# Relation lookups of a graph network on one Trainium2 core: one-hots in bfloat16 and a table in three bfloat16 parts

## The reference, cut to what matters

```python
half = N_REL // 2
is_fwd = edge_type < half
ridx = jnp.where(is_fwd, edge_type, edge_type - half)
for l in range(N_LAYERS):                       # 2 layers
    comp = x[src] * rel_emb[l][ridx]            # float32, 64 wide
    agg_f = jax.ops.segment_sum(comp * norm * fmask, dst, num_segments=N_NODES)
    agg_b = jax.ops.segment_sum(comp * norm * bmask, dst, num_segments=N_NODES)
    x = agg_f @ w_fwd[l] + agg_b @ w_bwd[l] + x @ w_loop[l]
    x = jax.nn.relu(x)
```

## Time and profile before

| | us |
|---|---|
| median of 3 runs | 11818.08 |
| lowest, highest | 11797.62, 11822.92 |
| the profiled execution's own time | 11901.01 |
| span of the program in it | 11899.2 |
| TensorE busy in the span (57%) | 6783.1 |
| GpSimd busy (51%) | 6085.0 |
| VectorE busy (36%) | 4232.3 |
| ScalarE busy (17%) | 1966.8 |

### The profile page before, as it was taken

The page is one execution under the profiler, slowest core; times in us unless marked ns, Lnnn a source line. Parts: engine busy times, 40 slices in busy tenths (PEclk is TensorE's granted clock), DMA queues, the critical chain, the costliest instruction groups (busy, mean ns, idle before and its releaser), DMA issues. The chain is left out here.

```text
span 11899.2 us, 136950 instructions
## 1 busy us (share of the span) xinstructions
PE 6783.1 (57%) x37299; PEld 5699.3 (48%) x37300; DVE 4232.3 (36%) x12350; ACT 1966.8 (17%) x5277; POOL 6085.0 (51%) x6396
## 2 busy tenths in 40 slices
PE   3554555556444445666666666676555555545454
PEld 3554544455322324555555555555455555444444
DVE  4333322222211113444444444444334333333333
ACT  1222200001211121111112111111211111111111
POOL 4666656665466653444443444444344444355554
PEclk6555556555667666666666666666655555566566
DMA  4444423232233322333332333333222222233333
GB/s 122 142 140 137 134 68 78 76 78 63 73 73 74 74 70 88 103 103 103 103 103 87 103 104 104 104 104 102 63 74 76 75 75 75 60 95 95 96 94 83
DMA packets 774628, 1092.78 MB, mean 92 GB/s; under 512 B 389184, under 2 KB 429440, under 8 KB 774160
## 3 DMA queue, kind: packets, MB, share of 16 engines
q0 software_dynamic: 233760, 503.07, 17.3%
q1 hardware_dynamic: 540784, 588.70, 16.5%
HBM read 1016.16 MB, written 75.04 MB: 92 GB/s over the span
## 5 line engine op out<-in xcount | busy, mean ns | idle before, releaser
L681 POOL DMA_INDIRECT gat_rows<-xw_table,gat_index x2736 | 2592.0, 947 | 3118.1 <-DVE gat_msg_s L1748 1971.9
L1834 PE MATMUL bank<-gat_msg_s,gat_hot 128*128 128x264 f32 (+1 forms) x5472 | 1942.7, 528 | 28.6 <-DVE gat_msg_s L1748 16.3
L1811 PE MATMUL bank<-gat_ends_s,gat_hot 128*128 128x9 f32 x5472 | 1153.2, 350 | 1183.1 <-issue 857.8
L1811 PEld LDWEIGHTS bank<-gat_ends_s,gat_hot 128*128 128x128 f32 x5472 | 1137.0, 316 | 1319.8 <-issue 950.0
L1834 PEld LDWEIGHTS bank<-gat_msg_s,gat_hot 128*128 128x128 f32 x5472 | 1430.8, 303 | 296.3 <-issue 31.0
L681 POOL DMA_INDIRECT att_rows<-pre_table,att_index x912 | 862.5, 946 | 830.1 <-ACT att_index L671 478.9
L681 POOL DMA_INDIRECT msg_rows<-pre_table,msg_index x912 | 864.8, 948 | 651.0 <-ACT msg_index L671 385.1
L681 POOL DMA_INDIRECT gcn_rows<-in_x,gcn_index x912 | 878.6, 963 | 573.8 <-ACT gcn_index L671 291.1
L681 POOL DMA_INDIRECT gcn_rows<-x_table,gcn_index x912 | 883.4, 969 | 554.4 <-issue 278.9
L893 PE MATMUL bank<-gcn_rel,gcn_rhot 100*128 100x64 f32 x3648 | 705.7, 347 | 792.4 <-issue 608.1
L730 PE MATMUL bank<-gcn_msg_s,gcn_hot 128*128 128x128 f32 x3648 | 844.9, 379 | 538.0 <-issue 530.4
(11 more groups left out here) (279 smaller groups left out, 8925.6 us busy)
## 6 DMA issues: line engine op xcount, KB each, us to landing
gcn_ids<-rel_rows SPq DMA_DIRECT2D x228, 400.0 KB
gat_hot_half<-edge_hots SPq DMA_DIRECT2D x342, 256.0 KB
gat_dhot<-dst_hots SPq DMA_DIRECT2D x342, 256.0 KB
gcn_dst<-dst_rows SPq DMA_DIRECT2D x114, 512.0 KB
gat_rows<-xw_table,gat_index POOLq DMA_INDIRECT x2736
edge_hots<-gcn_hot_half SPq DMA_DIRECT2D x114, 256.0 KB
dst_hots<-gcn_dhot SPq DMA_DIRECT2D x114, 256.0 KB
gcn_hot_half<-edge_hots SPq DMA_DIRECT2D x114, 256.0 KB
```

The source lines that it names most:

```text
L681: pool.indirect_dma_start(self.rows[n.q][:, j, :], None, self.table, bass.IndirectOffsetOnAxis(ap=self.index[n.q][:, j:j + 1], axis=0))\
L1811: ins = pe.matmul(pick_ps[:, j * (HEADS + 1):(j + 1) * (HEADS + 1)], hot[n.q][:, j, :], ends[q][:, j, :], start=True, stop=True)
L1834: ins = pe.matmul(sum_ps[g][:, 0:wide], hot[n.q][:, g * GROUP + j, :], msg[q][:, g * GROUP + j, :], start=j == 0, stop=j == GROUP - 1)
```

## The change

The relation one-hot `rhot` becomes bfloat16, in which zero and one are exact. The table `rel` is cut, once a pass, into three bfloat16 tiles whose sum is the float32 table: the first is `rel` rounded, the second what is left rounded, the third the rest. Each of the 8 products of a step becomes three bfloat16 products with the same one-hot, added up in PSUM. `PARTS` is 3.

```diff
-        rel = st.sb("rel", [HALF_REL, DIM])
+        rel_cut, rel_parted = st.sem("rel_cut"), st.sem("rel_parted")
+        rel, rel_rest = st.sb("rel", [HALF_REL, DIM]), st.sb("rel_rest", [HALF_REL, DIM])
+        rel_parts = st.sb("rel_parts", [HALF_REL, PARTS, DIM], BF16)
         ids = ring_sb(st, "ids", RING, [HALF_REL, BATCH * P])
-        rhot = st.pair_sb("rhot", [HALF_REL, BATCH * P])
+        rhot = st.pair_sb("rhot", [HALF_REL, BATCH * P], BF16)
...
                 dve.sem_inc(rel_hot, RING)
+                dve.wait_ge(rel_loaded, 16)
+                left, cuts = rel, 0
+                for k in range(PARTS):
+                    dve.tensor_copy(rel_parts[:, k, :], left[:, :]).then_inc(rel_cut, 1)
+                    cuts += 1
+                    dve.wait_ge(rel_cut, cuts)
+                    if k < PARTS - 1:
+                        dve.tensor_tensor(rel_rest[:, :], left[:, :], rel_parts[:, k, :], ALU.subtract).then_inc(rel_cut, 1)
+                        cuts += 1
+                        dve.wait_ge(rel_cut, cuts)
+                        left = rel_rest
+                dve.sem_inc(rel_parted, 1)
                 dve.sem_inc(comp_made, RING)
...
                     for j in range(BATCH):
-                        ins = pe.matmul(rel_ps[q][:, j * DIM:(j + 1) * DIM], rhot[q][:, j * P:(j + 1) * P], rel[:, :],
-                                        start=True, stop=True)
+                        for k in range(PARTS):
+                            ins = pe.matmul(rel_ps[q][:, j * DIM:(j + 1) * DIM], rhot[q][:, j * P:(j + 1) * P], rel_parts[:, k, :],
+                                            start=k == 0, stop=k == PARTS - 1)
...
-                pe.wait_ge(rel_loaded, 16)
+                pe.wait_ge(rel_parted, 1)
```

## The result

The changed kernel is slower. Its median is 11852.82 us (7 runs, 11845.37 to 11855.55) against 11804.03 us (7 runs, 11796.75 to 11822.92) of the kernel before beside it: ratio 1.0037, 95% interval 1.0025 to 1.0048, or some 49 us more (48.79). The profiled execution took 11854.37 us.

The account below looks back on a forecast made before the run. GpSimd's 10.0 us of gather issuing a step plus a standstill per run of two or three steps bounds the passes. 11901 - 23 + 2 = 11880 us profiled, less the 83 us offset: 11797 us; range 11640 to 11920, forecast's own 11770 to 11820.

Parts of the forecast that it names:

- The relation products: TensorE's products per step: 24 bfloat16 records take 1.1 us, 2.6 us less a step with clock down, 1 us with it up.
- How much of it is on the path: Share of TensorE's saving that shortens the relation passes, by lengthening some runs: 0.1 us a step, 23 us less over 228 steps.
- Rival B: TensorE's slow stretch comes after a number of instructions, so 40 records a step shorten runs: 45 to 95 us more; chance 0.25.
- The cutting of the table: Five VectorE instructions at each pass's start, ahead of the first one-hot: about 1.0 us a pass, 2 us more, not hidden.
- The one-hot on VectorE: L848 writing bfloat16 stays at 0.77 us; upper end 1214 ns, mostly hidden, otherwise 103 us more.
- the hold on GpSimd: VectorE's one-hot holds off GpSimd's gathers; ending that could win up to 42 us, but was counted as nothing.
- The offset of 83 us: Profiled execution lies 83 us above the plain runs' median; same offset taken from 11880 to reach 11797 us.
- Rivals A: Opening product counts in full, each run 2.4 us shorter: 216 us less, 11600, or 11710 for half the runs; chance 0.22.
- D: Nothing changes: run lengths stay and both stretches last what they did, 11820 us; chance 0.10.
- Rival C: Shorter products leave TensorE idle between sums, so its clock stays low: 50 us net of the 23, 11870; chance 0.07.
- My sign of being wrong: Forecast is wrong if either relation stretch moves by more than 40 us, or anything behind 2945 us changes length.

## Why the prediction was wrong

- *"The relation products ... I take 1.1 us."* Right in the middle: the 24 records of a group take 1.46 us with the clock down and 0.86 at the best, and all of them 205 us in pass 1.
- *"How much of it is on the path ... I take 0.1 us a step."* This is the step that failed, in its sign. I let the shorter product lengthen the runs, from two steps to three, and took 23 us off. They got shorter: runs of three steps went from 16 to 6 in pass 0 and from 25 to 20 in pass 1, and the 375 us that the quick stretches lost came back in full outside them. My picture had the quick stretch end at a time ("about 10 us"), so that shorter work would get more into it. It held 64 to 76 records in each stretch shown, of either length, and the change needs more of them for a step. I had also written that "in the slow stretch a shorter matmul buys nothing", for gaps of five times the record; the gap that I named is seven times (1.84 against 0.26 us), and records come at a quicker pace there when they are short (one in 0.79 us against 1.27), which did not make up for it.
- *Rival B* has the right place and sign, and its price (45 to 95) held the 49 us, but by luck: some 11 us of the 49 are the start, for which B had nothing, so that its own part is below 40. And it put 34 us on pass 1 and 10 (up to 60) on pass 0, where the traces have 4 and 13. I had given it 0.25 because the attention pass runs groups of 24 through without a gap; a group of 24 is well inside some 70 records and was no argument against. What is shown is that 8 more float32 records a step, with their time, cost 73 us. That three parts in bfloat16 cost nothing but their number at this level is argued from the unchanged one-hot and gathers, not shown, as one part was never seen there. Some 20 of the 49 us are not located in the two profiles.
- *"The cutting of the table ... 2 us more."* Mis-sized: the five instructions are 0.13 to 0.23 us each and end 1.0 us behind the MEMSET, as priced, but the credit that GpSimd's first gather needs stood behind them. In pass 1 that is 8.3 us, and 2.3 in pass 0; at the level of 8790 the kernel with the cutting alone measures 15 us (7 to 23 by the interval), the whole change 12 and 10. I named the one-hot and ScalarE as queued behind the cuts, and left out the sem_inc one line below, which had been handed out before the MEMSET began.
- *"The one-hot on VectorE ... I take 0.77."* Right, 0.76 us in pass 0 and 0.78 in pass 1 in the mean. The gathers' mean is 961 ns against 969, not the 947 that the end of the hold on GpSimd would have given, so little or nothing was won there.
- *The offset of 83 us.* It was that execution's own slowness, in unedited passes too; the profiled execution of the changed kernel lies 1.6 us from its median. The offset was right for before (11818 from 11901) and changes nothing in the sign, which came from the terms. The kernel before has 11804 over seven runs, 14 us below the 11818 that I counted from, so the forecast came to stand only 7 us below it.
- *Rivals A and D* are out by the sign and by the runs, which got shorter. *Rival C* is out: the granted clock of the stretches rose, from 0.59 and 0.58 to 0.62 and 0.60, and sums of 2.03 us still occur.
- *My sign of being wrong*, a stretch that moves by more than 40 us, did not come: from first to last gather they moved by 5 and 4 us, or by 13 and 4 with the slowness of the first profile taken out. It was too wide for a change of this size.

Stretches of the changed kernel (length, busy of each engine, PEclk, DMA), answering to the earlier trace rows:

```profile
90.00:1520.00 1430.00, 583.49 (x4562) 479.54 (x4563) 496.64 (x806) 379.65 (x457) 877.25 (x912) 0.62 0.48 138
1560.00:2960.00 1400.00, 590.54 (x4549) 485.52 (x4550) 364.68 (x686) 132.14 (x229) 876.47 (x912) 0.60 0.29 76
```

## What to carry to other kernels

Before new instructions go to the head of an engine's program, look for credits below them: a semaphore increment without an operand may leave ahead of the work that stands above it, and one wait put in front takes that away. Where an engine idles with "issue" in single records, count its instructions as well as its busy time; this change made a group's busy time less than half with half as many instructions more, and lost. And a profile tells of the chip it came from: this kernel has another bound on most of the chips seen, with 10.1 us a step set by the gathers, and there the versions with 24, 32 and 40 records a step can't be told apart.

## What the runs showed that I had not expected

The same kernel took 8790 to 8801 us on five chips and 11915.81 on a sixth. At the higher level TensorE falls into single records, mostly 0.7 to 2.8 us apart, 5 to 6 us behind GpSimd's restart in the mean with the bfloat16 products and 9 to 12 us with the float32 ones, and comes out of it 2.6 to 3.9 us (medians) after the last gather of a run; in the node stage behind pass 1, without gathers, no such stretch shows. At the lower level the same gathers, at the same 1.25 us apart, do nothing to it. Where the difference between the chips comes from I did not find in the traces. It is not that more code is loaded: the two instruction queues moved the same 40 and 44 packets in the kernel before at either level.
